# First offset convolution of each deformable layer in two parts, its first rows stored and arranged alone, and the PSUM banks of the transposes turned

## What is computed

```python
off = conv2d(x, ow, ob).reshape(Bn, K, 2, Hh, Ww)       # K = 9 taps, a y and an x offset each
cy = iy + dy + off[:, :, 0]; cx = ix + dx + off[:, :, 1]
y0, x0 = floor(cy), floor(cx); wy, wx = cy - y0, cx - x0
samp = gather(y0, x0, (1-wy)*(1-wx)) + gather(y0, x0+1, (1-wy)*wx) \
     + gather(y0+1, x0, wy*(1-wx)) + gather(y0+1, x0+1, wy*wx)
out = einsum('bckhw,ock->bohw', samp, w) + b
h = relu(group_norm1(out)) + x
```

## Time and profile before

| | us |
|---|---|
| median of 3 runs | 844.86 (841.74 to 846.12) |
| profiled execution | 836.0, its span 834.2 |
| TensorE matmuls busy | 633.1 (76% of the span) |
| VectorE busy | 592.5 (71%) |
| ScalarE busy | 461.6 (55%) |
| GpSimd busy | 148.8 (18%) |
| convolutions of both layers (L1291), busy | 85.9 in 2304 records |
| DMA moved | 108.73 MB, 130 GB/s over the span |

### The profile page before, as it was taken

How to read it: one execution, slowest core, us unless ns; L and a number is a source line. 1 busy time by engine, 2 the same in 40 slices (tenths; PEclk the granted TensorE clock), 3 DMA queues, 4 the chain that set the end, 5 groups by cost and what they waited for, 6 DMA issues and landing times.

```text
span 834.2 us, 30272 instructions
## 1 busy us (share of the span) xinstructions
PE 633.1 (76%) x13944; PEld 421.9 (51%) x13944; DVE 592.5 (71%) x823; ACT 461.6 (55%) x623; POOL 148.8 (18%) x219
## 2 busy tenths in 40 slices
PE   2506999999998757788888858867788888829392
PEld 1202555556886435655555636546655555617161
DVE  6794353112133599999999953699999999985465
ACT  3604343523233285888888532386888888451613
POOL 7000000000003412333331002433233331000000
PEclk9857999999999998999999979988999999969696
DMA  5000000000006787777775005797778873000002
GB/s 168 0 0 0 4 2 3 3 2 18 4 18 163 259 298 281 259 246 252 246 244 202 3 2 149 238 344 272 261 258 254 257 243 146 2 2 4 1 3 101
DMA packets 28778, 108.73 MB, mean 130 GB/s; under 512 B 10612, under 2 KB 15412, under 8 KB 24552
## 3 DMA queue, kind: packets, MB, share of 16 engines
q0 software_dynamic: 14400, 86.80, 31.0%
q1 hardware_dynamic: 14248, 19.97, 8.0%
HBM read 91.84 MB, written 19.65 MB: 134 GB/s over the span
## 4 chain that ended last, share of the span: by engine, by line
PE 47%; DVE 38%; ACT 7%; issue 5%; DMA 1%; SPq 0%; DVEq 0%; ACTq 0%
PE psum L1244 14%; PE psum L1291 9%; DVE arena L737 7%; DVE arena L738 7%; DVE arena L736 6%; PE psum L1324 5%; PE psum L1220 5%; PE psum L1347 5%; PE psum L1436 4%; DVE arena L420 4%; DVE arena L730 3%; PE psum L1303 2%; PE psum L1257 1%; PE psum L1443 1%; DVE arena L630 1%
## 5 line engine op out<-in xcount | busy, mean ns | idle before, releaser
L1324 PE MATMUL psum<-arena 64*64 64x297 f32 (+4 forms) x4512 | 221.9, 343 | 77.4 <-DVE arena L738 73.5
L1324 PEld LDWEIGHTS psum<-arena 64*64 64x64 f32 x4512 | 161.6, 134 | 137.4 <-DVE arena L738 85.1
L1506 POOL DMA_DIRECT2D arena<-offsets_by_batch x128 | 81.0, 648 | 220.1 <-DVE arena L738 155.8
L1096 ACT ACTIVATE arena<-psum 128x792 f32<-128x792 f32 (+1 forms) x96 | 84.6, 881 | 61.3 <-PE psum L1324 54.5
L1244 PE MATMUL psum<-arena 32*32 32x512 f32 x3456 | 115.1, 597 | 0.3 <-DVE arena L660 0.3
L1291 PE MATMUL psum<-arena 32*32 32x512 f32 x2304 | 85.9, 639 | 19.1 <-issue 13.3
L736 DVE SCALAR_TENSOR_TENSOR arena<-arena 128x792 f32<-128x792 f32 (+3 forms) x96 | 92.6, 965 | 4.2 <-ACT arena L1086 2.7
L1244 PEld LDWEIGHTS psum<-arena 32*32 32x32 f32 x3456 | 73.6, 103 | 39.8 <-issue 13.0
L738 DVE SCALAR_TENSOR_TENSOR arena<-arena 128x792 f32<-128x792 f32 (+3 forms) x96 | 92.2, 961 | 0.0
L737 DVE SCALAR_TENSOR_TENSOR arena<-arena 128x792 f32<-128x792 f32 (+3 forms) x96 | 92.2, 960 | 0.0
L1086 ACT ACTIVATE arena<-arena 128x792 f32<-128x792 f32 (+3 forms) x96 | 88.0, 917 | 0.0
(11 more groups left out here) (137 smaller groups left out, 701.6 us busy)
## 6 DMA issues: line engine op xcount, KB each, us to landing
arena<-offsets_by_batch POOLq DMA_DIRECT2D x112, 576.0 KB, 8.0
arena<-offsets_by_batch POOLq DMA_DIRECT2D x16, 624.0 KB, 7.8
offsets<-arena SPq DMA_DIRECT2D x32, 256.0 KB, 7.4
offsets_by_batch<-offsets SPq DMA_DIRECT2D x184, 24.0 KB
arena<-columns POOLq DMA_DIRECT2D x24, 160.0 KB, 9.3
columns<-arena POOLq DMA_DIRECT2D x8, 320.0 KB, 6.7
arena<-in_x SPq DMA_DIRECT2D x4, 512.0 KB, 5.4
out<-arena SPq DMA_DIRECT2D x8, 256.0 KB, 2.2
```

The lines of the kernel that those rows point to most:

```text
L1096: ins = a.activation(ap(SAMP + n // 2 % 2 * SPAR + n % 2 * SLOTS * K * SX + u * WB[0], [[SR, 2], [SX, KR], [1, w]]), ap_ps(bank, [[CH, 2], ...
L1324: ins = t_.matmul(ps_t(s, bank + r, first * K * w, many * K * w), window, ap(g_at(unit, d0) + first * TW + s * w, [[GS + TW, many], [SLOTS ...
L1506: g.dma_start(cols(in_at(n, 0), 2 * in_rows(n) * W, 64 * r + 32 * half, 32), bass.AP(batch_d.tensor, 2 * (4 * r * NB + n) * INS, [[0, QW / ...
```

## The change

`FIRST = 5` splits block 0 of each layer into rows 0 to 4 and rows 5 to 7 of each half (320 and 192 columns).

- TensorE: `convolve(0, 0, 5)` and `convolve(0, 5, 8)` take the place of `convolve(0)`, 144 matmuls each; the first goes to banks 4 to 7, the second to banks 0 to 3, and the other blocks swap theirs (1 and 3 in banks 4 to 7, 2 in 0 to 3). The wait for all of the layer's input stands between the parts. The turned groups go in the order 4, 5, 6, 7, 0, 1, 2, 3; the first of each four waits until the part that used its bank has been copied out.
- ScalarE: eight copies instead of four for block 0; the wait for all of the input ahead of them is gone. VectorE: block 0 is bounded in two parts, four instructions instead of two.
- SP: stores rows 0 to 4 of half 0 with 2 DMAs, arranges batch 0 (its wait is for these 2 alone), and then stores the rest of block 0 with 4 DMAs; arrange 1 and 2 follow.
- POOL: the first part of `store_columns` waits for all 4 + 4 groups; batch 1 is loaded ahead of `load_windows(1)`.

```diff
+FIRST = 5
-        def conv_bank(m):
-            return 4 if m % 2 == 0 else 0
+        def conv_bank(m, first=0):
+            return 0 if m % 2 == 0 and m + first > 0 else 4
+        def written(L, m, end=CR):
+            return 20 * L + 4 * m + (8 if m or end == CR else 4)
+        def stored(L, m):
+            return (64 if m else 96) * (L + 1)
             def arrange_batch(L, n):
-                sp.wait_ge(s_ds[min(SLOTS * n + SLOTS, H - 1) // BLK], 64 * (L + 1))
+                m = min(SLOTS * n + SLOTS, H - 1) // BLK
+                sp.wait_ge(s_ds[m], stored(L, m) if n else 96 * L + 32)
             for L in range(2):
+                sp.wait_ge(s_d1, 5 * L + 1)
+                store_rows(0, 0, 0, FIRST)
+                arrange_batch(L, 0)
                 store_offsets(L, 0)
-                arrange_batch(L, 0)
                 arrange_batch(L, 1)
...
-                bound_offsets(L, 0)
-                for g_ in (1, 3, 5, 7):
+                bound_offsets(L, 0, 0, FIRST)
+                bound_offsets(L, 0, FIRST, CR)
+                for g_ in (5, 7, 1, 3):
                     copy_columns(L, g_)
...
-                act.wait_ge(s_xa, NCH * (L + 1))
-                copy_offsets(L, 0)
-                for g_ in (0, 2, 4, 6):
+                copy_offsets(L, 0, 0, FIRST)
+                copy_offsets(L, 0, FIRST, CR)
+                for g_ in (4, 6, 0, 2):
                     copy_columns(L, g_)
...
-                convolve(0)
+                convolve(0, 0, FIRST)
                 pe.wait_ge(s_xa, NCH * (L + 1))
-                for g_ in range(8):
-                    if g_ == 4:
-                        pe.wait_ge(s_cve, 16 * L + 4)
+                convolve(0, FIRST, CR)
+                for g_ in (4, 5, 6, 7, 0, 1, 2, 3):
+                    if g_ % 4 == 0:
+                        pe.wait_ge(s_cve, written(L, 0, FIRST if g_ else CR))
                     turn_columns(g_)
...
-                groups = (3, 2) if part == 0 else (4, 4)
-                pool.wait_ge(s_xta, 4 * L + groups[0])
-                pool.wait_ge(s_xtv, 4 * L + groups[1])
+                pool.wait_ge(s_xta, 4 * L + 4)
+                pool.wait_ge(s_xtv, 4 * L + 4)
...
                 load_batch(L, 0)
+                load_batch(L, 1)
                 load_windows(L, 1)
-                load_batch(L, 1)
```

More of the change, by code:

```diff
@@ L224, in ps, with ps_q @@
             return psum[0:pn, bank, off:off + n]
-        def ps_q(quadrant, bank):
-            return psum[quadrant * Q:(quadrant + 1) * Q, bank, 0:CH]
+        def ps_q(quadrant, bank, off=0, n=CH):
+            return psum[quadrant * Q:(quadrant + 1) * Q, bank, off:off + n]
         def ps_t(half, bank, off, n):
@@ L448, in store_offsets, with store_rows @@
             def store_offsets(L, m):
-                sp.wait_ge(s_d1, 4 * L + m + 1)
+                sp.wait_ge(s_d1, 5 * L + m + 2)
+                for h in range(2):
+                    store_rows(m, h, FIRST if m == h == 0 else 0, CR)
+            def store_rows(m, h, first, end):
                 for axis in range(2):
[L452 to L456, removed]
+                    sp.dma_start(bass.AP(off_d.tensor, axis * B * KP * N + (2 * m + h) * CH + first * W,
+                                         [[N, 2 * KP], [2 * KP * N, 4], [1, (end - first) * W]]),
+                                 ap(D1 + m % 2 * NATS + first * W, [[CH, 4], [1, (end - first) * W]],
+                                    64 * axis + Q * h, Q)).then_inc(s_ds[m], 16)
             def arrange_batch(L, n):
-                sp.wait_ge(s_ds[min(SLOTS * n + SLOTS, H - 1) // BLK], 64 * (L + 1))
+                m = min(SLOTS * n + SLOTS, H - 1) // BLK
+                sp.wait_ge(s_ds[m], stored(L, m) if n else 96 * L + 32)
                 if n >= 4:
@@ L699, in copy_columns, with bound_offsets @@
             def copy_columns(L, g_):
-                dve.wait_ge(s_tp, 8 * L + g_ + 1)
+                dve.wait_ge(s_tp, 8 * L + (g_ + 4) % 8 + 1)
                 v.tensor_copy(ap(XT + 4 * g_ * C, [[C, 4], [H // 2 * C, B], [1, C]]),
                               ap_ps(g_, [[P, 4], [C, B], [1, C]])).then_inc(s_xtv, 1)
-            def bound_offsets(L, m):
-                dve.wait_ge(s_cve, 16 * L + 4 * m + 4)
+            def bound_offsets(L, m, first=0, end=CR):
+                dve.wait_ge(s_cve, written(L, m, end))
                 if m >= 2:
[L709 to L714, removed]
+                    dve.wait_ge(s_ds[m - 2], stored(L, m - 2))
+                rows = lambda at, pn: ap(at + m % 2 * NATS + first * W, [[CH, 4], [W, end - first], [1, W]], 0, pn)
+                link(v.tensor_scalar(rows(D1, P), rows(RAW, P), con("minus_limit"), con("limit"), ALU.max, ALU.min))
+                v.tensor_tensor(rows(D1, 64), rows(D1, 64),
+                                ap(CON + CONST["ramp"][0], [[0, 4], [0, end - first], [1, W]], 0, 64),
+                                ALU.add).then_inc(s_d1, 1)
             def reach(L, m):
@@ L1056, in copy_columns, with copy_offsets @@
             def copy_columns(L, g_):
-                act.wait_ge(s_tp, 8 * L + g_ + 1)
+                act.wait_ge(s_tp, 8 * L + (g_ + 4) % 8 + 1)
                 a.activation(ap(XT + 4 * g_ * C, [[C, 4], [H // 2 * C, B], [1, C]]),
                              ap_ps(g_, [[P, 4], [C, B], [1, C]]), ACT.Copy).then_inc(s_xta, 1)
-            def copy_offsets(L, m):
+            def copy_offsets(L, m, first=0, end=CR):
                 if m >= 2:
                     act.wait_ge(s_red, 4 * L + m - 1)
-                    act.wait_ge(s_d1, 4 * L + m - 1)
+                    act.wait_ge(s_d1, 5 * L + m)
+                at, n = first * W, (end - first) * W
                 for i in range(4):
-                    act.wait_ge(s_cv, 16 * L + 4 * m + i + 1)
-                    a.activation(cols(RAW + m % 2 * NATS + i * CH, CH), ps(conv_bank(m) + i, 0, CH), ACT.Identity,
+                    act.wait_ge(s_cv, written(L, m, end) - 3 + i)
+                    a.activation(cols(RAW + m % 2 * NATS + i * CH + at, n), ps(conv_bank(m, first) + i, at, n), ACT.Identity,
                                  bias=cols(OB + L, 1)).then_inc(s_cve, 1)
@@ L1132, in _ @@
                         for m in range(4):
-                            act.wait_ge(s_ds[m], 64 * (L + 1))
+                            act.wait_ge(s_ds[m], stored(L, m))
                         act.wait_ge(s_red, 4 * (L + 1))
@@ L1282, in _, with convolve @@
             for L in range(2):
-                def convolve(m):
+                def convolve(m, first=0, end=CR):
                     pe.wait_ge(s_xa, NCH * L + max(min(2 * m + 3, NCH), 4))
@@ L1290, in convolve @@
                                 for h in range(2):
-                                    ins = t_.matmul(ps_q(2 * axis + h, conv_bank(m) + i),
+                                    ins = t_.matmul(ps_q(2 * axis + h, conv_bank(m, first) + i, first * W, (end - first) * W),
                                                     cols(W_CONV[L] + (axis * K + t) * Q, Q, Q * i, Q),
-                                                    ap(XA + (BLK * m + 8 * h + t // 3 + 1) * XW + t % 3 + 1,
-                                                       [[XW, CR], [1, W]], Q * i, Q),
+                                                    ap(XA + (BLK * m + 8 * h + first + t // 3 + 1) * XW + t % 3 + 1,
+                                                       [[XW, end - first], [1, W]], Q * i, Q),
                                                     start=(t == 0), stop=(t == K - 1))
@@ L1369, in _ @@
                 convolve(2)
-                pe.wait_ge(s_cve, 16 * L + 8)
+                pe.wait_ge(s_cve, written(L, 1))
                 convolve(3)
-                pe.wait_ge(s_cve, 16 * (L + 1))
+                pe.wait_ge(s_cve, written(L, 3))
                 pe.wait_ge(s_ws, 16)
```

## The result

The changed kernel takes 852.5 us (median of 4, 850.76 to 854.14), the one before 843.3 us beside it: ratio 1.0109, 95% interval 1.0065 to 1.0153, so 9 us slower. Its profiled execution has a span of 850.4 us against 834.2.

The account below looks back on a forecast made before the run. TensorE's list up to block 2's bounding, then VectorE, was taken to bound each layer. Terms +1.9 + 1.0 - 2.6 - 0.8 + 1.0 = +0.5 us on the median 844.86 gave 845.4 us, range 838.5 to 852.5.

Parts of the forecast that it names:

- B: Rival, slower: second part's records held to instruction issue pace; 852.5 us at 17.5 ns a record, 862 at 33.1; chance 0.27.
- A: Main case, no change: 845.4 us, by its bounds about 840.8 to 849; chance 0.50, Rival D included.
- milder form: Form of B: A's record price plus one more late packet per layer, DMA being full sooner; 850.4 us, chance 0.18.
- What bounds: Each layer's start-up: TensorE's list up to block 2's bounding sets the layer; batch 0's road has 2.6 and 0.3 us slack.
- Step 1: TensorE, block 0: 288 more records at 6.7 ns beside their columns; +1.9 us in layer 0, +1.0 in layer 1.
- Step 2: TensorE's instruction packets: stops come 32 pairs earlier; -2.6 us in layer 0, -0.8 and +1.0 (block 3) in layer 1.
- bounds of (1) and (2): Limits on Step 1, 0 to 5.0 us a layer, and on Step 2, -2.5 to +2.5 us.
- Step 3 and 4: Waits between parts and before turned groups, no cost; ScalarE's four and VectorE's two more instructions in idle time, nothing.
- Step 5: SP: batch 0's issues some 10 us sooner, rest of block 0 stored later; nobody on the bounding road waits.
- Step 6: POOL: later turned-image store; batch 0's load leaves 2 us sooner than 275.35, not 10; batch 1 about 10 us sooner.
- Rival D: POOL's windows go first, so batch 0 lands at most 2 us sooner, or later in layer 1; 846.6 us, inside A.

Follow-up runs that it names:

- e1: Against before, only TensorE's records changed: block 0 convolved in parts of 320 and 192 columns into the old banks; ratio 1.0163, 854.7 us beside 842.4.
- e2: Against before, the change without TensorE's and ScalarE's part: block 0 convolved whole, bounded in two parts, early store and arrangement, POOL's part; ratio 0.9962.
- e4: As e1, but block 0 split at row 7, into 448 and 64 columns; ratio to before 1.0206.
- e3: Against before, POOL's part alone: first turned-image store waits for all eight groups, batch 1 loaded ahead of window rows 9 to 16; ratio 0.9959, 838.3 us.
- e8: The kernel of e3 measured once more against before, both POOL edits and nothing else; ratio 0.9944, 838.4 us.

## Why the prediction went as it did

I forecast no change, 845.4 us; it is 9 us slower, at the very end of the range. The case that came is B, slower, which I had given 0.27, but in neither of its forms. Its 852.5 us came from a record at 17.5 ns, with the stops as in A, and its milder form had the late packets come from full DMA. That 852.5 us was also measured is luck: the records cost 3.3 and 1.8 us directly, half of the 10.0 us that B gave them, and late packets the rest, the first of them with idle DMA.

- **What bounds** (block 2's bounding sets the layer): held for before's layer 0 and nearly for e1, where B less A is 198.7 to 199.2 us. "The layer ends a fixed time after" did not hold in general: from the clipping of block 2 to the aggregate it was 198.0 and 198.2 us in the first trace of before, but 202.8 us in layer 1 of the second, behind a wait for batch 0, and 200.1 and 201.6 us in the two layers of the change, where VectorE waits up to 2.4 and 3.58 us for a third unit.
- **Step 1, the price of a record**, +1.9 and +1.0 us: mis-sized, by 1.4 and 0.8 us. In layer 0 block 0 grew by 5.2 us. Of that 2.0 are stops; the 320-column records take 7.8 us busy and the 192-column ones 18.2 ns each (128 in 2.33 us), 5.2 us in all, 13.0 us together against my 11.4. So the direct price was 3.3 us. In layer 1 block 0 grew by 4.2 us (16.1 against 11.9), 2.4 of it stops, so 1.8 directly.
- **Step 2, "two more boundaries fall into block 0, where DMA is idle, at no cost"**: the step that failed. I had read from rows 5 and 9 that a low DMA share means no stop. It means none at 33 ns a pair: 128 pairs then last 4.2 us. With 192 columns they last 2.3 us, and the runs started 3.5 to 4.0 us apart (252.20, 255.66, 259.40 in the change; 251.25, 255.26, 259.27 in e1), each behind its packet, with a DMA share of 0.20 in that stretch of the change and of 0.01 in e1's. The stretches of after and then of e1, with the columns of rows 5:

```profile
251.00:258.00 7.00, 5.04 (x270) 3.46 (x248) 2.43 (x2) 1.43 (x5) 0.00 (x0) 1.00 0.20 52
```

```profile
251.00:259.00 8.00, 5.56 (x256) 4.08 (x256) 0.00 (x0) 1.86 (x4) 0.00 (x0) 1.00 0.01 4
```

  TensorE is busy 5.56 of 8.00 us at full clock, with next to nothing on the DMA engines.

- **Step 2, the stops behind it**: that they stand a multiple of 128 pairs apart held. That they come 32 pairs sooner held in layer 0 alone. Layer 0's own 288 more pairs count for layer 1 too, so there they come 64 sooner: the boundary that I moved from 41 to 12 pairs into block 3, "still behind block 2", landed before the end of block 2 and stopped TensorE for 3.95 us on the road that bounds. I had misread the counts of layer 0 as well: rows 3 give 174, 301 and 557 pairs, not 190, 318 and 574, so the last stop had 19 pairs of block 2 left and not one or two. My 3.3 us up to block 2 in layer 0 came out as 0.75 us, the -2.6 us as -5.1; in layer 1 my -0.8 came out as +3.8 (2.53 and 3.95 instead of 2.70). The lengths could not be read off one trace.
- **The range of A**: the bounds of (1) and (2), added, give 840.0 to 855.0 us and not 840.8 to 849; with them A would have held the measured time.
- **Step 3 and 4** (waits between the parts, ScalarE and VectorE): held, as far as the product of e1 and e2 tells. VectorE's idle time before block 1 was 9.8 us.
- **Step 5**: "nobody on the bounding road waits for them" was wrong in kind: in e2 VectorE waits 4.89 and 6.74 us for the late store. In the change itself TensorE is later still and hides it.
- **Step 6**: batch 0 was to leave at 273.3 and left at 280.09, since the turned groups ended six us later after the layer's first record. ScalarE's wait for it was to be gone and was 5.72 us; VectorE's first instruction of batch 0 waited 0.2 us. Rival D was thus true as far as it went: the early arrangement brought batch 0 no sooner.
- **The Trainium skill**, TensorEngine Tiling (Array Packing), Instruction Overhead: the estimate of 14.4 us in all that I drew from it is nearer to e1's +14 us (1.0163 of 842) than my sum was, but not for its reason. I had counted records; by its words a matmul has the overhead, which makes 144 a layer and an estimated 7.2 us in all. The 64-column pairs of e4 go out at 11.8 ns, under half of 60 cycles at full clock, and what held them was the packet behind.

## What to carry to other kernels

Count TensorE's instructions, not its columns, when a convolution is cut: here a run of 128 pairs that is over sooner than the next packet arrives (3.5 to 4.0 us) waits for it, even with DMA nearly idle, and the kernel before, with 4.2 us a run, stood just above that pace. Count on from the start of the program: instructions added in one layer move the boundaries of all that follow, here by 32 pairs in layer 0 and by 64 in layer 1. Splitting an accumulation by output rows doubles the instructions of that block and buys earliness only if a transfer, not TensorE, comes last. A slack of 0.3 us in one trace is no slack: take a second trace of the same kernel before building on it.

## What the runs showed of the hardware that was not expected

TensorE's instruction packets set its pace with idle DMA: 3.47 us between the starts of two runs of 64-column pairs (e4: 513.93, 517.40) and 3.5 to 4.0 us for 192 columns, with a DMA share down to 0.01. In e1's stretch a packet leaves 1.2 to 1.7 us after a run has begun, takes 0.9 us, and the next run begins 1.4 to 1.6 us after that. With full DMA the same boundary cost between nothing and 4.17 us, and starting a store of 2 MB about 2 us later together with another order of two loads took away 0.5% of the kernel (e3, e8), while the same edits one by one gave +0.4% and nothing. That makes it likely that where the packets fall among the loads decides; it was not isolated.
